# A decoder with a routed mixture: row and product transposes side by side on TensorE, rows turned two pairs ahead, and separate sum arrays for even and odd pairs

## The reference

```
idx = top_k(router_scores + expert_bias, 8);  w = scores at idx, divided by their sum
g = einsum('th,ehi->tei', t, Wg);  u = einsum('th,ehi->tei', t, Wu)
act = silu(g) * u
moe = einsum('tei,te,eih->th', act, wfull, Wd)
shared = silu(t @ Wsg) * (t @ Wsu) @ Wsd
return resid + (moe + shared)
```

## Time and profile before

| | us |
|---|---|
| median of 3 runs | 2481.89 (2481.78 to 2491.12) |
| profiled execution | 2484.49 |
| its span | 2482.7 |
| TensorE busy in the span | 2247.6 (91%) |
| VectorE busy | 1295.4 (52%) |
| ScalarE busy | 934.5 (38%) |
| POOL busy | 912.4 (37%) |

### The profile page before, as it was taken

One profiled execution on the slowest core, in us unless ns is written; L12 is line 12 of the kernel. 1 busy time (PEld: TensorE's weight loads), 2 busy tenths in 40 slices (PEclk: granted clock), 3 DMA queues, 4 the chain that ended last, 5 costly groups with the idle time before them and its releaser, 6 DMA issues. The chain is left out here.

```text
span 2482.7 us, 41946 instructions
## 1 busy us (share of the span) xinstructions
PE 2247.6 (91%) x15664; PEld 1597.8 (64%) x15664; DVE 1295.4 (52%) x2342; ACT 934.5 (38%) x1630; POOL 912.4 (37%) x723
## 2 busy tenths in 40 slices
PE   7889999688999998889999799778879999979997
PEld 6658787567888887533333233266657777759997
DVE  4563666647777777443233232376762666643333
ACT  1332222334454543236665466113642323222221
POOL 2333111355655564215655455353433101012220
PEclk9999999899999999989999899888999999969999
DMA  3011000222121210446656677720011000011110
GB/s 121 23 64 55 27 27 2 73 78 71 39 69 39 69 39 1 163 134 159 138 136 156 170 210 209 195 88 25 2 56 58 31 18 26 1 51 52 51 51 30
DMA packets 53009, 186.58 MB, mean 75 GB/s; under 512 B 8196, under 2 KB 8452, under 8 KB 45956
## 3 DMA queue, kind: packets, MB, share of 16 engines
q1 hardware_dynamic: 35540, 145.09, 17.2%
q0 software_dynamic: 17280, 38.94, 8.1%
HBM read 155.03 MB, written 28.97 MB: 74 GB/s over the span
## 5 line engine op out<-in xcount | busy, mean ns | idle before, releaser
L2031 PE MATMUL bank<-m_ring,m_bT 128*64 x576 | 266.3, 606 | 7.6 <-ACT m_upper L1777 3.4
L2033 PE MATMUL bank<-m_upper,m_bT 128*64 128x512 f32 x576 | 266.5, 606 | 0.0
L1958 DVE SCALAR_TENSOR_TENSOR m_prod<-bank,m_slot_rows,m_silu 64x256 f32<-64x256 f32 x144 | 69.6, 484 | 266.7 <-ACT m_silu L1722 264.1
L2031 PEld LDWEIGHTS bank<-m_ring,m_bT 128*64 128x64 f32 x576 | 73.9, 138 | 146.8 <-issue 146.8
L1777 ACT ACTIVATE m_upper<-m_ring 128x1024 f32 x144 | 143.3, 1043 | 14.9 <-DMA m_ring<-in_m_w 14.2
L2060 PE MATMUL bank<-m_ring,m_aT 128*64 x288 | 140.7, 611 | 7.2 <-DVE m_aT L1974 7.2
L832 ACT ACTIVATE y_att_p_rows<-bank,y_att_n_top 112x375 f32<-112x375 f32 x128 | 71.7, 573 | 193.6 <-DVE y_att_n_top L874 193.6
L1689 POOL DMA_INDIRECT m_sum<-m_yb,m_idx x72 | 102.9, 1429 | 105.8 <-DMA m_sum<-m_yb,m_idx 78.0
L2062 PE MATMUL bank<-m_upper,m_aT 128*64 128x512 f32 x288 | 140.7, 611 | 0.0
L1681 POOL DMA_INDIRECT m_slot_rows<-m_rows,m_idx x72 | 72.7, 1010 | 144.2 <-DVE m_prod L1958 96.6
L829 ACT ACTIVATE x_att_pT<-x_att_s_clip 125x336 f32<-125x336 f32 x128 | 55.3, 486 | 170.2 <-DVE x_att_s_clip L868 170.2
(11 more groups left out here) (494 smaller groups left out, 6136.8 us busy)
## 6 DMA issues: line engine op xcount, KB each, us to landing
m_ring<-in_m_w SPq DMA_DIRECT2D x32, 1536.0 KB
f_raw<-in_f_wq SPq DMA_DIRECT2D x64, 256.0 KB, 2.6
z_raw<-in_z_w SPq DMA_DIRECT2D x7, 1536.0 KB
f_att_wo_raw<-in_f_wo SPq DMA_DIRECT2D x16, 512.0 KB, 6.2
x_c_raw<-in_ctxT SPq DMA_DIRECT2D x8, 752.0 KB, 4.6
y_c_raw<-in_ctxT SPq DMA_DIRECT2D x8, 752.0 KB, 4.2
m_sum<-m_slot_rows SPq DMA_DIRECT2D x2, 2048.0 KB, 15.0
a_raw<-in_a_wqk SPq DMA_DIRECT2D x8, 256.0 KB, 8.5
```

The lines of the kernel that those rows point to most:

```text
L2031: pe.matmul(ps_gu[u % 2][0:HP, :], bT[:, n % 2, k, 0:HP], ring[:, bass.ds(slot + at, D)], start=(k == 0), stop=(k == KC - 1))
L2033: o = pe.matmul(ps_gu[u % 2][HP:P, :], bT[:, n % 2, k, HP:P], upper[:, n % 2, at:at + D], start=(k == 0), stop=(k == KC - 1))
```

## The change

TensorE does the down products of pair n - 1 right behind gate/up of pair n, then the four row transposes, now of pair n + 2, and then the two product transposes. The rows get a fourth buffer (NR). ScalarE's copies of the turned rows move accordingly. There are four sum arrays: even pairs add into 0 and 1, odd pairs into 2 and 3, and from pair 62 on (TAIL = 10) all into 0 and 1. SyncE fetches arrays 2 and 3 into y and x2 behind its wait for all ring loads, and VectorE adds them to x, two batch elements behind each of the pairs 68 to 71 (`add_odd`). The final fetch of arrays 0 and 1 waits for these additions.

```diff
@@ SyncE
-            for i in range(2):
+            for i in range(4):
                 sp.dma_start(sums_dram[i].rearrange("(a p) d -> p a d", p=P),
                              zero[:, 0:D].unsqueeze(1).broadcast_to([P, TROWS // P, D])).then_inc(sums_set, 16)
...
             sp.wait_ge(ring_in, 16 * E_MOE)
+            for i, into in ((2, y), (3, x2)):
+                sp.wait_ge(summed[i], 16 * pairs_in(i // 2, NBLK))
+                sp.wait_ge(x_done, B)
+                sp.dma_start(into[:, :, :], sums_dram[i][0:T, :].rearrange("(b s) d -> s b d", b=B)).then_inc(odd_in, 16)
             for i, into in ((0, y), (1, x2)):
-                sp.wait_ge(summed[i], 16 * NBLK)
-                if i == 1:
-                    sp.wait_ge(x_done, B)
+                sp.wait_ge(summed[i], 16 * pairs_in(0, NBLK))
+                if i == 0:
+                    sp.wait_ge(odd_done, B)
@@ POOL
             def gather(n):
-                if n >= 3:
-                    pool.wait_ge(prod_done, FRONT + n - 2)
-                    pool.wait_ge(bt_done, n - 2)
-                pool.indirect_dma_start(rows[:, n % 3, :], None, rows_dram[:, :],
+                if n >= NR:
+                    pool.wait_ge(prod_done, FRONT + n - NR + 1)
+                    pool.wait_ge(bt_done, n - NR + 1)
+                pool.indirect_dma_start(rows[:, n % NR, :], None, rows_dram[:, :],
...
             def scatter(n):
                 pool.wait_ge(yb_done, n + 1)
-                if n:
-                    pool.wait_ge(summed[0], 16 * n)
...
+                at = sums_of(n)
+                for i, places in ((2 * at, idx[0:HP, n:n + 1]), (2 * at + 1, upper_idx[:, n:n + 1])):
+                    if pairs_in(at, n):
+                        pool.wait_ge(summed[i], 16 * pairs_in(at, n))
+                    pool.indirect_dma_start(sums_dram[i][:, :], bass.IndirectOffsetOnAxis(ap=places, axis=0),
+                                            yb[halves[i % 2], n % 2, :], None, compute_op=ALU.add).then_inc(summed[i], 16)
@@ new
+NR = 4
+TAIL = 10
+        def sums_of(n):
+            return n % 2 if n < NBLK - TAIL else 0
+        def pairs_in(at, n):
+            return sum(sums_of(m) == at for m in range(n))
@@ ScalarE
             collect_rows(0)
+            collect_rows(1)
...
                 silu_of(FRONT + n)
                 if n + 1 < NBLK:
-                    collect_rows(n + 1)
                     copy_upper_down(n + 1, slot)
+                if n + 2 < NBLK:
+                    collect_rows(n + 2)
@@ VectorE
             def collect_y(n):
                 dve.wait_ge(dn_done, FRONT + n + 1)
                 if n >= 2:
-                    dve.wait_ge(summed[0], 16 * (n - 1))
-                    dve.wait_ge(summed[1], 16 * (n - 1))
+                    at = sums_of(n - 2)
+                    dve.wait_ge(summed[2 * at], 16 * pairs_in(at, n - 1))
+                    dve.wait_ge(summed[2 * at + 1], 16 * pairs_in(at, n - 1))
...
+            def add_odd(b):
+                dve.wait_ge(odd_in, 32)
+                dve.wait_ge(x_done, B)
+                if b < FRONT:
+                    dve.wait_ge(add_done, b + 1)
+                dve.tensor_tensor(x[:, b, :], x[:, b, :], y[:, b, :], ALU.add).then_inc(odd_first, 1)
+                dve.wait_ge(odd_first, b + 1)
+                dve.tensor_tensor(x[:, b, :], x[:, b, :], x2[:, b, :], ALU.add).then_inc(odd_done, 1)
             for n in range(NBLK):
                 prod_block(n)
                 if n:
                     collect_y(n - 1)
                 collect_block(n)
+                if n >= NBLK - 4:
+                    for b in range(2 * (n - NBLK + 4), 2 * (n - NBLK + 4) + 2):
+                        add_odd(b)
@@ TensorE
             turn_rows(0)
+            turn_rows(1)
...
                 gate_up_halves(n, slot)
-                if n + 1 < NBLK:
-                    turn_rows(n + 1)
                 if n:
                     down_halves(n - 1, slot_before)
+                if n + 2 < NBLK:
+                    turn_rows(n + 2)
                 turn_a(FRONT + n)
```

More of the change, by code:

```diff
@@ L1582, in moe @@
         upper_idx = sb("upper_idx", [HP, NBC], I32)
-        rows = sb("slot_rows", [P, 3, HR])
+        rows = sb("slot_rows", [P, NR, HR])
         zero = rows[:, 2, :]
@@ L1612, in moe @@
         late_in = [sem(f"late_in{h}") for h in range(B // 2)]
-        rows_in = [sem(f"rows_in{i}") for i in range(3)]
-        summed = [sem(f"summed{i}") for i in range(2)]
+        rows_in = [sem(f"rows_in{i}") for i in range(NR)]
+        summed = [sem(f"summed{i}") for i in range(4)]
+        odd_in, odd_first, odd_done = map(sem, ("odd_in", "odd_first", "odd"))
         (zero_set, c16_done, aggr_done, sq_done, ms_done, rrms_done, y_done, tr_done, hT_done, x_done) = map(sem, (
@@ L1677, in gather @@
             def gather(n):
-                if n >= 3:
-                    pool.wait_ge(prod_done, FRONT + n - 2)
-                    pool.wait_ge(bt_done, n - 2)
-                pool.indirect_dma_start(rows[:, n % 3, :], None, rows_dram[:, :],
+                if n >= NR:
+                    pool.wait_ge(prod_done, FRONT + n - NR + 1)
+                    pool.wait_ge(bt_done, n - NR + 1)
+                pool.indirect_dma_start(rows[:, n % NR, :], None, rows_dram[:, :],
                                         bass.IndirectOffsetOnAxis(ap=idx[:, n:n + 1], axis=0)
-                                        ).then_inc(rows_in[n % 3], 16)
+                                        ).then_inc(rows_in[n % NR], 16)
             def scatter(n):
                 pool.wait_ge(yb_done, n + 1)
-                if n:
-                    pool.wait_ge(summed[0], 16 * n)
[L1689 to L1694, removed]
+                at = sums_of(n)
[4 more added lines that the diff above has]
+                                            yb[halves[i % 2], n % 2, :], None, compute_op=ALU.add).then_inc(summed[i], 16)
             pool.memset(zero, 0.0).then_inc(zero_set, 1)
@@ L1706, in _ @@
             pool.wait_ge(share_set, 16)
-            pool.wait_ge(sums_set, 32)
+            pool.wait_ge(sums_set, 64)
             for n in range(3):
@@ L1817, in add_shared @@
                 dve.wait_ge(x_done, b + 1)
+                if b >= FRONT:
+                    dve.wait_ge(odd_done, b + 1)
                 dve.tensor_tensor(x[:, b, :], ps_d[u % 2][0:S, :], x[:, b, :], ALU.add).then_inc(add_done, 1)
@@ L1958, in prod_block @@
                     p = dve.scalar_tensor_tensor(prod[now, u % 2, :], ps_gu[u % 2][now, EI:2 * EI],
-                                                 rows[now, n % 3, bass.ds(expert[i] + D, 1)], silu[now, u % 2, :],
+                                                 rows[now, n % NR, bass.ds(expert[i] + D, 1)], silu[now, u % 2, :],
                                                  ALU.mult, ALU.mult)
@@ L2151, in turn_rows @@
             def turn_rows(n):
-                pe.wait_ge(rows_in[n % 3], 16 * (n // 3 + 1))
+                pe.wait_ge(rows_in[n % NR], 16 * (n // NR + 1))
                 if n >= 2:
@@ L2155, in turn_rows @@
                 for k in range(KC):
-                    t = pe.transpose(ps_t[n % 2][:, k * P:(k + 1) * P], rows[:, n % 3, k * P:(k + 1) * P], g.const("ident"))
+                    t = pe.transpose(ps_t[n % 2][:, k * P:(k + 1) * P], rows[:, n % NR, k * P:(k + 1) * P], g.const("ident"))
                 t.then_inc(bt_done, 1)
@@ L2450, in program @@
         m_rows = nc.dram_tensor("m_rows", (TROWS, HR), F32).ap()
-        m_sums = [nc.dram_tensor(f"m_sum{i}", (TROWS, D), F32).ap() for i in range(2)]
+        m_sums = [nc.dram_tensor(f"m_sum{i}", (TROWS, D), F32).ap() for i in range(4)]
         loaded = nc.alloc_semaphore("loaded")
```

## The result

The changed kernel took 2505.64 us, median of 5 runs (2499.72 to 2512.62); the kernel before took 2481.89 in the same comparison (5 runs, 2479.25 to 2491.12). The profiled execution took 2499.72 us, with a span of 2497.9.

A forecast was written before the change was run, and what follows sets the result against it. The period was taken as bound by the silu, VectorE product and slot-load chain, the stage's end by transfers. The final fetch 30.6 us later made 2484.49 into 2515.1 profiled, 2512 as median; range 2503 to 2521.

The forecast's parts named there:

- The order gains nothing: Steady pairs: the chain through silu, VectorE's product and slot load keeps the period at 6.43 us despite TensorE's shorter work.
- the products set the period after all: Rival for the steady pairs: TensorE's own work sets the period, bringing the time to 2492 us; chance 0.08.
- What the freed 0.35 us a pair would be worth, 20 us: TensorE in steady pairs: bound on the other side, 0.35 us for each of some 58 pairs, 20 us.
- Shifts of load 23, -0.5: SyncE's ring load 23: three small shifts, +1.0, -0.75 and -0.75, sum to -0.5 us, issued at about 1509.6.
- Shift (a): Before the loop: turning pair 1's rows there puts a copy and four transposes ahead of gate/up 0, +1.0 us.
- shift (c): Ring load 23 waits for down products, which now start right behind gate/up, earlier in the pair: -0.75 us.
- Ring steps of 7.97: SyncE's ring loads 23 to 31: eight steps of 7.97 us each, then 6.9 us until load 31 lands at 1580.3.
- Fetch of the odd sums, 17.0: SyncE's fetches behind all ring loads take 17.0 us, so the odd sums land at 1597.5.
- The stall, 42: VectorE reaches its wait for the odd sums after pair 68 at about 1555 and stands about 42 us.
- From the landing to the even fetch, 27.4: Stage end: additions and pairs 69 to 71 take 27.4 us from the odd sums' landing to the final fetch's issue.
- Gathers and zeroing, nothing: Gathers have 8.2 us of cover, and zeroing two more arrays (10 us) fits idle queues before the loop: no cost.
- The sum: Final fetch of the even sums issued at 1624.9 instead of 1594.25, 30.6 us later; median predicted 2512 us.

The follow-up runs named there:

- Order alone: Kernel before with TensorE's new order, rows two pairs ahead and a fourth rows buffer, two sum arrays: 2483.56 us, ratio 1.0019.
- the early rank in the old order: Kernel before with one edit, TensorE reading the next pair's rank and slot ahead of the product transposes: 2477.1 us, ratio 0.9988.
- early fetch: Changed kernel with the odd arrays fetched from ScalarE's queue at pair 64: ratio 1.0007; with the rank also read ahead of the product transposes: 0.9931.
- two-array kernels of the new order: Kernel before with new order and four rows buffers: ratio 1.0019; the same with the rank read ahead of the product transposes: 0.9964.
- additions behind the loop: Changed kernel with VectorE's 16 additions of the odd sums moved behind the last pair: 2493.55 us, ratio 1.0048 to the kernel before.
- 24 loads: Changed kernel with 24 in place of 32 ring loads, leaving out experts without tokens: 2468.12 us, ratio 0.9944 to the kernel before.
- arrays alone: Changed kernel with the old order on TensorE and three rows buffers, four sum arrays kept: 2515.0 us, ratio 1.0135 to the kernel before.

## Why the prediction was right, point by point

- **The order gains nothing**: right, and for the reason given. Order alone gave 1.0019; with the rank load out of the chain the period fell to 6.11, for a forecast of 6.08 by TensorE's work alone. Pair 0's 3.38 us had told the two apart. The idle time ahead of gate/up was 0.20 to 0.24 us, for 0.35. The rival *the products set the period after all* was half true: in the old order they set it too, 0.03 us away, as the early rank in the old order shows.
- **What the freed 0.35 us a pair would be worth, 20 us**: the freed time was 0.30 (6.41 to 6.11). 1.0007 to 0.9931 between the two kernels with the early fetch is 19 us. Between the two-array kernels of the new order, 1.0019 to 0.9964, it is 14, and 8 of them against the kernel before, as late gathers and the scatters at the end took the rest.
- **Shifts of load 23, -0.5**: it was issued at 1503.70, 6.4 earlier than in the profiled execution before. A good part of that is no effect of the change. From gate/up 0 to load 23 that execution took 417.6 us, but the kernel before without the last eight loads, whose code is the same up to there, took 414.2; the changed kernel and its three variants that are the same up to there (additions behind the loop, 24 loads, early fetch) took 410.9 to 412.7. So the change brought something between 1.4 and 6.7 us, and the profiled pair stands at the far end of both. The old order with four arrays took 412.8 and the order alone 416.8, so what gain there is seems to go with the arrays and not with the order. Shift (a) was 0.3 us at gate/up 0 for 1.0; shift (c) is in the rows of pair 32, where the last down piece starts 4.77 us into the pair (1304.37) for a forecast of 4.78. The prediction had the shorter stall for the ring (11.9 us for 14.21) at 0.75, and nothing for the arrays in the loop; which wait of the loop they shorten stays open.
- **Ring steps of 7.97**: 7.52 ((1563.84 - 1503.70) / 8). This too is mostly spread: the step was 7.96 with the additions behind the loop, 7.93 with the arrays alone and 7.45 with the order alone. With load 23, load 31 landed at about 1570.5 and not at 1580.3. The two make 5.9 + 3.6 of these 9.8 us, most of what the forecast was too high in this execution's stage.
- **Fetch of the odd sums, 17.0**: 16.1 (1570.5 to 1586.6). The price of 10 to 12 by the fit in the Trainium skill, "DMA: Bandwidth & Descriptors", on the anatomy of one DMA (given there for transfers that GpSimd issues), does not hold for this transfer.
- **The stall, 42**: 34.6 us. The sums landed 10.9 us earlier than forecast, and VectorE reached the wait 3.0 earlier, at 1552.0.
- **From the landing to the even fetch, 27.4**: 29.3. The lower clock lasted longer than in rows 9: 5.58 us from gate/up 70's first piece to its last, for 4.63, and product 69 came 0.75 after the additions and not 0.54.
- **Gathers and zeroing, nothing**: right. TensorE's waits for rows come to 5.6 us on its weight loads and 2.1 on its matmuls from pair 0 to the end of the stage, 3.7 of the former in pairs 66 and 67. That four arrays would be useless below pair 62 was right for the time only at a period of 6.4; at 6.11 they are worth about 0.12 us a pair.
- **The sum**: 30.6 us later for the even fetch, 21.6 measured, that is 10.9 less for the landing of the odd sums and 1.9 more for the chain behind it. The mechanism stood as forecast: fetch behind the loads, VectorE's wait, product 69 behind it, and each member from the landing to the even fetch. What was off is a size, the time at which load 31 lands, and it was worked out from the one profiled execution before, whose load 23 was late and whose ring steps were long by the spread shown above. So the time was forecast to rise by 30 us and rose by 24. The median lies in the lower part of the range of 2503 to 2521; the stage's 21.6 us alone would have put it at 2503.5, on the range's end.

## What to carry to other kernels

When an engine is busy for 99.8% of a steady stretch, look for a second chain of the same length before you reorder its work: here register work on the queue stood behind a semaphore wait, and neither edit gave anything that could be told until both were made. A transfer that someone waits for must not be queued behind waits that have nothing to do with it, and its price is also paid by what runs beside it. A term that is read from one profiled execution carries that execution's spread; a second one would have shown it here. A wait put into an engine's program holds everything behind it, so put it where nothing that others need follows.

## What the runs showed of the hardware

- A register load on TensorE's queue behind the product transposes starts 0.05 us after the end of VectorE's product that they wait for, in every pair of the kernel before and in all but two of the changed one, and the next gate/up comes 1.11 to 1.16 us after that in most pairs, 1.17 to 1.6 in the others. Read one step earlier in the queue, it leaves the period at TensorE's own work (6.11 and 6.41 us in the two orders).
- The chain of indirect scatter-adds, each waiting for the one before, takes 4.3 to 4.4 us a pair alone, mostly 7.1 to 8.6 beside ring loads of 1.5 MB and 8.1 to 8.7 beside the 3.67 MB fetch.
- A wait of 2.4 us on TensorE was followed by matmul steps of 0.75 to 0.91 us in place of 0.43 (granted clock 0.57 over 4 us, so mostly the lower level, 1.2 GHz); after the 33 us hole six steps took 0.83 to 0.90.
